# Four graph layers on one core: normalization moved to ScalarE, biases added within the gathering passes, and another order in the attention loop

## The chip, the cores and the metric

One NeuronCore of one Trainium2 chip. The time is that of one execution on the device, in microseconds (us). The kernel before took 5311.9 us, the median of three runs (5303.4 to 5312.3).

## The reference, cut to what matters

Four graph layers on 6,250 nodes with 128 features and 100,000 edges sorted by `dst`, each followed by a layer norm of x plus the layer's result:

```python
x = _layernorm(x + gat(x, ...))     # attention: softmax over the edges of each dst, weighted sum of h[src]
x = _layernorm(x + cfconv(x, ...))  # filters from edge_attr_128, messages, segment sum, two dense layers
x = _layernorm(x + gcn(x, ...))     # normalized sum of neighbours, + bias
x = _layernorm(x + gin(x, ...))     # (sum of neighbours + x) through two dense layers, + bias

def _layernorm(x, eps=1e-05):
    return (x - mean(x)) / sqrt(var(x) + eps)

# cfconv
f = ssp(edge @ We1 + be1) @ We2 + be2        # ssp(x) = softplus(x) - log 2
agg = segment_sum(xn[edge_index[1]] * f, edge_index[0])
return node + ssp(agg @ W2 + b2) @ W3 + b3   # so x + this = 2*node + ... + b3
```

## The kernel before, in words

Each engine has its own program (`vector`, `scalar`, `tensor`, `gpsimd`, `sync`), an in-order list of instructions; semaphores tie them together. The order of all work is written out by hand: a loop over ticks t, in which each engine works on several items, each with a lag behind t.

The nodes lie in 49 blocks of 128, the edges in 832 steps of up to 128 edges that share a block; four steps are a tick, so a pass over the edges has 208 ticks (`TICKS`). For the normalizing stages the blocks are grouped in 13 sets of four (`SETS`, `NS`; the last set has one block).

**Attention loop** (L802 to 815, L1155 to 1166, L1419 to 1428). GpSimd gathers rows of the table into a ring of 14 ticks (L1606 to 1612) and waits for `product_done` of 14 ticks earlier. VectorE has in each tick: `gat_top` (L663, the maximum of TensorE's masked bank), every fourth tick the chains `gat_max` (L673) and `gat_logit` (L715), `gat_sum` (L751, four dependent sums into `acc`), `gat_hot` (L742), `gat_turn` (L655), one or two steps of a background sort (`second_list`, L773), and last `f_plus_of` (L767), the sum that ends the softplus of the edge filters of the next layer. `weave` (L103) goes round these pieces, one step of each in a round, with a background step in the first and every third round. ScalarE has the background first, then `gat_dst`, `gat_weight`, `f_made_of`, `gat_weigh` and last `f_soft` (absolute value, exponential, logarithm). TensorE has the background first, then `gat_pair`, `gat_product`, `gat_mask`, `f_filter` and `f_hidden_of`. The filter chain is a ring over three engines: `f_hidden_of` (TensorE) waits for the last `f_plus_of`, `f_soft` for `f_hidden_of`, `f_plus_of` for `f_soft`.

At 14 places the background sort turns its keys over: TensorE transposes four 128x128 tiles into bank 3 (L1268), ScalarE copies them out (L1027), TensorE transposes four more after that copy, ScalarE copies again. On both engines that is one background step, so TensorE's second four stand at the head of its tick and wait for ScalarE's first copy. For the first 49 ticks ScalarE also counts in the background (L1015).

**Normalizing stages.** Per set, VectorE makes x plus the layer's result (`res`, a ring of four), its statistics (`stats_of`, L824) and later (lag 2) the normalization itself, `normed` (L832), one tensor_scalar per block; ScalarE makes 1/sqrt(var + eps) (`root`, L1168) as exponential of a logarithm. In stage 1 (L843) and stage 3 (L966) VectorE first adds the layer's bias row to x for the whole set (L850, L973). In stages 2 (L924) and 4 (L988) the result comes from two dense layers through TensorE and ScalarE (`turn`, `keep`, `times`, softplus or relu), and the bias of the second one is put into its bank by a matmul of a row of ones (L1444). In stage 1 TensorE then makes the table of the message stage from x, in stage 2 that of the third layer; stage 3's x goes to memory as the table of the fourth layer (L1794), and stage 4's is the output.

**The passes of layers 2 to 4** (`plain_layer`: L875, L1491, L1624). GpSimd gathers four times a tick, VectorE makes the hot blocks (L884), TensorE multiplies (L1498), VectorE adds the four products to the blocks' rows of `acc` (L872).

## Time and profile before

| | us |
|---|---|
| median of three runs | 5311.9 |
| the profiled execution | 5312.5 |
| its span, first to last instruction | 5310.7 |
| attention loop | 188 to 1391 |
| stage 1, normalization | 1391 to 1447 |
| message stage | 1447 to 1940 |
| pass of layer 2 | 1940 to 3003 |
| stage 2 | 3003 to 3072 |
| pass of layer 3 | 3072 to 4137 |
| stage 3 | 4137 to 4191 |
| pass of layer 4 | 4191 to 5257 |
| stage 4 | 5257 to 5311 |

Over the whole span TensorE's matmuls are busy 2721 us, VectorE 2760, ScalarE 1320, GpSimd 3525. These are averages over stages with different limits, so they name no limit of the whole. In rows of the trace, L12 is line 12 of the kernel, an arrow `<-` in brackets tells what ended the idle time before an instruction, PE is TensorE (PEld its weight loads), DVE VectorE, ACT ScalarE, POOL GpSimd. Instructions of a kind that follow each other closely stand in one row with their count (x4).

### The profile page before, as it was taken

How to read it: one execution, taken by the hardware profiler on the slowest of the kernel's cores; microseconds unless marked ns; L12 is line 12 of the kernel's file. 1: busy time of each engine (PE TensorE's matmuls, PEld its weight loads, DVE VectorE, ACT ScalarE, POOL GpSimd, SP SyncE). 2: the span in 40 equal slices, each digit the busy share in tenths (PEclk: the TensorE clock that was granted, in tenths of full speed). 3: DMA queues.
4: the chain of work that ended last, by engine and by line, in shares of the span. 5: the costliest groups of instructions: out<-in, count | busy, mean ns of one | idle time of the engine just before them, and what ended most of it. 6: DMA issues, size and time to landing. Idle time of an engine off the chain costs nothing. (4 is left out here: it accounts for less than half of the span.)

```text
span 5310.7 us, 54159 instructions
## 1 busy us (share of the span) xinstructions
PE 2721.2 (51%) x13301; PEld 2238.2 (42%) x13381; DVE 2760.1 (52%) x7383; ACT 1319.8 (25%) x3951; POOL 3524.7 (66%) x3833
## 2 busy tenths in 40 slices
PE   1477767777588864443333644434443244444445
PEld 1356555556466653333333433333333133333333
DVE  2699888888788863333333533333333533333334
ACT  4587666667366630000000200000000000000001
POOL 0677666767255557777777467777777377777773
PEclk8798898989677765555555655555555555555556
DMA  4666666667376742221111122212223222222224
GB/s 75 175 168 166 150 155 157 161 155 172 33 227 221 230 151 53 53 53 51 52 51 50 40 61 53 52 50 53 53 53 51 52 53 52 51 52 52 53 53 50
DMA packets 430927, 489.97 MB, mean 92 GB/s; under 512 B 86459, under 2 KB 333071, under 8 KB 430614
## 3 DMA queue, kind: packets, MB, share of 16 engines
q0 software_dynamic: 131904, 288.49, 23.2%
q1 hardware_dynamic: 295828, 197.27, 13.4%
q8 instruction: 116, 1.90, 0.2%
q10 hardware_dynamic: 2882, 0.70, 0.1%
q14 instruction: 197, 1.61, 0.1%
HBM read 359.63 MB, written 126.50 MB: 92 GB/s over the span
## 5 line engine op out<-in xcount | busy, mean ns | idle before, releaser
L1498 PE MATMUL bank<-arena 128*128 128x128 f32 x4992 | 1277.1, 438 | 1968.8 <-DVE arena L884 1690.8
L1572 POOL DMA_INDIRECT arena<-node_table,pick x1664 | 1593.0, 957 | 650.7 <-issue 507.2
L1498 PEld LDWEIGHTS bank<-arena 128*128 128x128 f32 x4992 | 1111.4, 328 | 2134.3 <-DVE arena L884 1863.8
L872 DVE TENSOR_TENSOR acc<-acc,bank 128x128 f32 x2496 | 719.1, 288 | 2101.7 <-PE bank L1498 1810.5
L1572 POOL DMA_INDIRECT arena<-gat_table,pick x832 | 856.3, 1029 | 348.2 <-issue 237.4
L1572 POOL DMA_INDIRECT arena<-message_table,pick x832 | 803.9, 966 | 255.8 <-issue 253.3
L1179 ACT COPY xt<-bank 128x512 f32<-128x512 f32 (+1 forms) x39 | 21.6, 554 | 2131.8 <-PE bank L1438 2131.7
L884 DVE TENSOR_TENSOR arena<-iota_free,local 128x512 f32<-128x512 f32 x624 | 428.0, 686 | 3.4 <-issue 2.4
L1487 PE MATMUL bank<-arena 128*128 x1664 | 338.4, 367 | 46.9 <-DVE arena L898 40.7
L1487 PEld LDWEIGHTS bank<-arena 128*128 128x128 f32 x1664 | 290.2, 263 | 114.2 <-issue 114.2
L763 DVE SCALAR_TENSOR_TENSOR acc<-acc,arena,bank 128x129 f32 x832 | 287.4, 345 | 66.0 <-DVE acc L763 34.1
L1171 ACT ACTIVATE rstd<-moments,eps_col 128x4 f32<-128x4 f32 (+1 forms) x52 | 15.5, 299 | 1158.3 <-DVE moments L829 1158.1
L1202 ACT ACTIVATE arena<-arena 128x128 bf16<-128x128 f32 x832 | 257.7, 310 | 153.6 <-DVE arena L906 133.8
L1391 PEld LDWEIGHTS bank<-arena 128*128 128x128 f32 x1664 | 260.3, 229 | 78.4 <-issue 70.1
L1391 PE MATMUL bank<-arena 128*128 128x129 f32 x1664 | 275.0, 318 | 7.5 <-ACT arena L1127 4.1
L1127 ACT ACTIVATE arena<-arena 128x128 f32<-128x128 f32 x832 | 265.4, 392 | 34.4 <-DVE arena L746 34.4
L1648 POOL DMA_DIRECT2D arena<-filter_table x208 | 112.5, 541 | 228.7 <-DVE arena L898 176.8
L1408 PE MATMUL bank<-xt,w_L_gnn_We 128*128 128x512 f32 x262 | 156.1, 680 | 189.5 <-DVE arena L769 188.7
L1400 PEld LDWEIGHTS bank<-w_L_gnn_We,arena 128*128 128x128 f32 x1568 | 219.3, 202 | 17.4 <-issue 7.0
L1400 PE MATMUL bank<-w_L_gnn_We,arena 128*128 128x128 f32 x1568 | 216.8, 283 | 11.6 <-ACT arena L1149 5.8
L898 DVE TENSOR_TENSOR arena<-bank,arena 128x512 f32<-128x512 f32 x208 | 143.8, 691 | 85.4 <-PE bank L1487 77.5
L769 DVE SCALAR_TENSOR_TENSOR arena<-bank,neg_L_gnn_be,arena 128x512 f32<-128x512 f32 x196 | 146.1, 746 | 79.5 <-ACT arena L1143 78.7
(219 smaller groups left out, 3373.2 us busy)
## 6 DMA issues: line engine op xcount, KB each, us to landing
message_table<-arena POOLq DMA_DIRECT2D x208, 256.0 KB, 3.3
filter_table<-arena SPq DMA_DIRECT2D x196, 256.0 KB
arena<-filter_table SPq DMA_DIRECT2D x624, 64.0 KB
xt<-edge_cols SPq DMA_DIRECT2D x131, 256.0 KB
arena<-local_rows SPq DMA_DIRECT2D x208, 128.0 KB
arena<-node_table,pick POOLq DMA_INDIRECT x1664
arena<-edge_cols SPq DMA_DIRECT2D x65, 256.0 KB
arena<-gat_table,pick POOLq DMA_INDIRECT x832
```

The costliest lines, as they stand in the source:

```text
L763: e.scalar_tensor_tensor(a, a, small["scale"][:, g % 2, q + s:q + s + 1], sum_place(t, s), ALU.mult, ALU.add).then_inc(summed, 1)
L769: e.scalar_tensor_tensor(magn[u % 2][:, :], bank[0][:, :], neg_col["L1_gnn_be1"][:, 0:1], magn[u % 2][:, :], ALU.max, ALU.add).then_inc(f_ ...
L872: e.tensor_tensor(a, a, bank[6 + t % 2][:, s * P:(s + 1) * P], ALU.add).then_inc(sums, 1)
L884: e.tensor_tensor(hot[n % 2][:, :, :], iota_free[:, :].unsqueeze(1).to_broadcast([P, GRP, P]), local[which][:, i:i + GRP].unsqueeze(2).to_ ...
L1127: ins = e.activation(hot[t % 3][:, s, :], hot[t % 3][:, s, :], ACT.Copy, scale=weight[:, s:s + 1])
L1202: e.activation(hot_copy[:, :], hot_n[n % HN][:, s * P:(s + 1) * P], ACT.Copy, accum_out=degree_part[:, i:i + 1]).then_inc(degree_added, 1)
L1391: ins = e.matmul(sum_place(t, s), hot[t % 3][:, s, :], gathered[:, slot(t, s), 0:D + 1], start=True, stop=True)
L1400: ins = e.matmul(bank[1][:, s * P:(s + 1) * P], magn[u % 2][:, s * P:(s + 1) * P], mats["L1_gnn_We2"][:, :], start=True, stop=True)
L1408: e.matmul(bank[0][:, :], mats["L1_gnn_We1"][:, :], edge_t[u % 3][:, :], start=True, stop=True).then_inc(f_hidden, 1)
L1487: ins = e.matmul(spread_bank(n)[:, s * P:(s + 1) * P], hot_n[n % HN][:, s * P:(s + 1) * P], xn[:, bass.ds(b, 1), :].rearrange("p o d -> p ...
L1498: ins = e.matmul(bank[6 + n % 2][:, s * P:(s + 1) * P], hot[n % 2][:, s, :], gathered[:, slot(n, s), 0:D], start=True, stop=True)
L1572: e.indirect_dma_start(out=dst, out_offset=None, in_=table, in_offset=bass.IndirectOffsetOnAxis(ap=index, axis=0)).then_inc(done, 16)
```

## The change

- `normed` moves from VectorE to ScalarE in all four stages: out of (res - mean) * rstd becomes Identity(res * rstd + shift), with shift = -mean * rstd made by VectorE for the whole set (`shift_of`, in the place where `normed` was, one 128x4 operation). The lags of what follows grow by one tick in stages 1 and 2.
- The bias rows of layers 2, 3 and 4 are added to x by VectorE within the pass before the stage that needs them (`add_row`, one operation per set, every eighth tick from tick 4). For layer 2 it is half of the row, since the stage takes x twice. The bias matmuls of stages 2 and 4 and the bias addition of stage 3 go. The first layer's bias addition (L850) stays.
- As x now changes within the last pass, VectorE waits for the writes of the fourth layer's table before it begins that pass.
- Attention loop: `f_plus_of` is a piece of `weave`, with one empty step first, so that it comes behind the second sum; ScalarE's tick begins with `f_soft` and `f_made_of`, and the background comes last. TensorE's tick is as before.

```diff
@@ vector, setup
-            e.tensor_tensor(out_row[:, :], bank[4][:, P:2 * P], rows["L1_gnn_b3"][:, :], ALU.add
-                            ).then_inc(fold_taken, 1)
+            q = own(e.tensor_tensor(out_row[:, :], bank[4][:, P:2 * P], rows["L1_gnn_b3"][:, :], ALU.add))
+            after(q)
+            e.tensor_scalar(half_row[:, :], out_row[:, :], 0.5, None, ALU.mult).then_inc(fold_taken, 1)
@@ vector, attention loop
             def f_plus_of(u):
+                yield
                 e.wait_ge(f_log, u + 1)
...
+                if 0 <= t - 3 < FTICKS:
+                    pieces.append(f_plus_of(t - 3))
                 weave(pieces, background, background_turns(t))
-                if 0 <= t - 3 < FTICKS:
-                    run(f_plus_of(t - 3))
@@ vector, normalizing stages
-            def normed(n, rs, x):
+            def shift_of(n, rs):
+                b0, b1 = span(n)
                 e.wait_ge(rs, n + 1)
-                for k, b in enumerate(SETS[n]):
-                    ins = e.tensor_scalar(x_sb[:, b, :], res[n % 4][:, k, :], moments[:, b, 0:1], rstd[:, b:b + 1],
-                                          ALU.subtract, ALU.mult)
-                ins.then_inc(x, 1)
+                e.scalar_tensor_tensor(shift[:, b0:b1], moments[:, b0:b1, 0], -1.0, rstd[:, b0:b1], ALU.mult, ALU.mult
+                                       ).then_inc(shifted, 1)
+
+            def add_row(n, row):
+                b0, b1 = span(n)
+                return own(e.tensor_tensor(x_sb[:, b0:b1, :], x_sb[:, b0:b1, :],
+                                           row[:, :].unsqueeze(1).to_broadcast([P, b1 - b0, D]), ALU.add))
...
-            def plain_layer(which, base):
+            def plain_layer(which, base, row):
                 for t in range(TICKS + 4):
+                    if t % 8 == 4 and t // 8 < NS:
+                        added = add_row(t // 8, row)
...
                 e.wait_ge(plain_summed, base + STEPS)
+                after(added)
...
@@ vector, stage 3 and the pass of layer 4
-                    q = own(e.tensor_tensor(xb[n % 2][:, 0:b1 - b0, :], x_sb[:, b0:b1, :],
-                                            rows["L2_gnn_b"][:, :].unsqueeze(1).to_broadcast([P, b1 - b0, D]),
-                                            ALU.add))
-                    after(q)
...
-                                                       xb[n % 2][:, k, :], ALU.mult, ALU.add))
+                                                       x_sb[:, b, :], ALU.mult, ALU.add))
...
-            plain_layer(0, 2 * STEPS)
+            e.wait_ge(table_out, 2 * 16 * NS)
+            plain_layer(0, 2 * STEPS, rows["L3_gnn_b2"])
@@ scalar, attention loop
             for t in range(TICKS + 13):
-                weave([], background, background_turns(t))
+                for lag, fn in ((3, f_soft), (5, f_made_of)):
+                    if 0 <= t - lag < FTICKS:
+                        fn(t - lag)
                 for lag, fn in ((4, gat_dst), (9, gat_weight)):
                     if (t - lag) % GT == 0 and 0 <= t - lag < TICKS:
                         fn((t - lag) // GT)
-                for lag, fn in ((5, f_made_of), (10, gat_weigh), (3, f_soft)):
-                    if 0 <= t - lag < (TICKS if fn is gat_weigh else FTICKS):
-                        fn(t - lag)
+                if 0 <= t - 10 < TICKS:
+                    gat_weigh(t - 10)
+                weave([], background, background_turns(t))
@@ scalar, normalizing stages
+            def normed(n, stage, x):
+                e.wait_ge(shifted, stage * NS + n + 1)
+                for k, b in enumerate(SETS[n]):
+                    ins = e.activation(x_sb[:, b, :], res[n % 4][:, k, :], ACT.Identity, scale=rstd[:, b:b + 1],
+                                       bias=shift[:, b:b + 1])
+                ins.then_inc(x, 1)
...
-            for t in range(NS + 8):
-                n = t - 7
+            for t in range(NS + 9):
+                n = t - 8
...
+                n = t - 3
+                if 0 <= n < NS:
+                    normed(n, 0, n1_x)
...
@@ tensor, times
-            def times(n, bk, buf, mat, done, bias_row=None):
-                cnt = len(SETS[n])
-                if bias_row is not None:
-                    e.matmul(bk[:, 0:cnt * P], ones[0:1, :], bias_row[0:1, :].unsqueeze(1).to_broadcast([1, cnt, D]),
-                             start=True, stop=False)
-                for k in range(cnt):
+            def times(n, bk, buf, mat, done):
+                for k in range(len(SETS[n])):
                     ins = e.matmul(bk[:, k * P:(k + 1) * P], buf[n % 2][:, k * P:(k + 1) * P], mat[:, :],
-                                   start=bias_row is None, stop=(bias_row is None or k == cnt - 1))
+                                   start=True, stop=True)
```

ScalarE's `normed` stands at lag 8 in stage 2, 3 in stage 3 and 8 in stage 4; the other shifted lags follow the diff's pattern.

## Rows read from the trace of the kernel before

**Rows 1.** Stages: length, busy us (count) of PE, PEld, DVE, ACT, POOL; clock, DMA share, GB/s

```profile
188.00:1391.00 1203.00, 855.44 (x5544) 697.62 (x5624) 1017.82 (x2713) 820.55 (x1942) 833.70 (x810) 0.89 0.66 155
1391.00:1447.00 56.00, 26.54 (x149) 22.21 (x149) 49.64 (x212) 18.71 (x52) 10.40 (x21) 0.70 0.10 27
3040.00:3050.00 10.00, 10.00 (x62) 7.09 (x61) 8.91 (x32) 6.66 (x16) 0.00 (x0) 1.00 0.17 52
4137.00:4191.00 54.00, 0.00 (x0) 0.00 (x0) 50.65 (x212) 12.91 (x39) 0.23 (x1) 0.50 0.20 60
5257.00:5311.00 54.00, 45.54 (x199) 26.41 (x199) 36.20 (x160) 21.34 (x52) 0.00 (x0) 0.88 0.20 60
```

**Rows 2.** Timeline in a pass: start, length, engine, line, operation [idle before <- its end]

```profile
2240.08 0.94 POOL L1572 DMA_INDIRECT arena<-message_table,pick  x1 [0.30 <-issue]
...
2244.92 0.29 DVE L872 TENSOR_TENSOR acc<-acc,bank 128x128 f32 x1 [2.80 <-PE bank L1498]
```

**Rows 3.** Timeline, an ordinary tick of the attention loop

```profile
603.23 1.06 PE L1391 MATMUL bank<-arena 128*128 128x129 f32 x8
...
605.99 0.35 DVE L763 SCALAR_TENSOR_TENSOR acc<-acc,arena,bank 128x129 f32 x1 [0.15 <-DVE acc L763]
...
606.26 0.74 DVE L769 SCALAR_TENSOR_TENSOR arena<-bank,neg_L_gnn_be,arena 128x512 f32<-128x512 f32 x1
...
606.92 0.68 DVE L666 TENSOR_REDUCE arena<-bank 128x4 f32<-128x512 f32 x1
```

**Rows 4.** Waits in the attention loop: waiting <- releaser: us in total, times, longest

```profile
DVE arena L769 <- ACT arena L1143: 78.7, 40, 5.7
```

**Rows 5.** Timeline, the first turn of the sort, and the last one's wait

```profile
540.73 0.58 ACT L1027 COPY arena<-bank 128x512 f32<-128x512 f32 x1 [5.90 <-PE bank L1268]
541.37 0.66 PE L1268 MATMUL bank<-ident,arena 128*128 128x128 f32 x4 [0.68 <-ACT arena L1027]
...
544.21 0.68 ACT L1139 ACTIVATE arena<-bank,c_L_gnn_be 128x512 f32<-128x512 f32 x1
...
546.24 0.75 DVE L769 SCALAR_TENSOR_TENSOR arena<-bank,neg_L_gnn_be,arena 128x512 f32<-128x512 f32 x1 [5.50 <-ACT arena L1143]
546.68 1.28 ACT L1127 ACTIVATE arena<-arena 128x128 f32<-128x128 f32 x4
...
547.14 1.63 PE L1408 MATMUL bank<-arena,w_L_gnn_We 128*128 128x512 f32 x2 [2.16 <-DVE arena L769]
...
548.56 1.93 PE L1391 MATMUL bank<-arena 128*128 128x129 f32 x8
...
1108.15 0.75 DVE L769 SCALAR_TENSOR_TENSOR arena<-bank,neg_L_gnn_be,arena 128x512 f32<-128x512 f32 x1 [5.67 <-ACT arena L1143]
```

**Rows 6.** Waits of GpSimd in the attention loop, and its last one, by timeline

```profile
POOL arena L1572 <- PE bank L1391: 97.4, 52, 5.7
...
1176.88 0.94 POOL L1572 DMA_INDIRECT arena<-gat_table,pick  x1 [4.43 <-PE bank L1391]
```

**Rows 7.** Timeline, VectorE's work for one set in stage 3

```profile
4152.52 0.69 DVE L973 TENSOR_TENSOR arena<-x_sb,r_L_gnn_b 128x512 f32<-128x512 f32 x1
4153.24 1.14 DVE L980 SCALAR_TENSOR_TENSOR arena<-acc,inv_sqrt_deg,arena 128x128 f32<-128x128 f32 x4
4154.41 0.87 DVE L826 BATCH_NORM_STATS2 stats<-arena 128x6 f32<-128x128 f32 x4
4155.32 0.38 DVE L829 BATCH_NORM_AGGREGATE moments<-stats 128x2 f32<-128x6 f32 x4
4155.62 1.08 DVE L835 TENSOR_SCALAR x_sb<-arena,moments,rstd 128x128 f32<-128x128 f32 x4
```

**Rows 8.** Groups by line, VectorE in the attention loop: count | busy us, mean ns | idle before

```profile
L684 DVE SCALAR_TENSOR_TENSOR arena<-arena 128x16 f32<-128x16 f32 x52 | 8.6, 165 | 0.0
```

**Rows 9.** Timeline, VectorE's first work of the message stage

```profile
1446.93 2.07 DVE L906 TENSOR_SCALAR arena<-bank,iota_part 128x512 f32<-128x512 f32 x3 [5.01 <-PE bank L1474]
```

**Rows 10.** Timeline, a bias matmul of stage 4

```profile
5283.42 1.12 PE L1444 MATMUL bank<-r_L_gnn_b,ones 1*128 1x512 f32 x2
```

More of the change, by code:

```diff
@@ L202, in build_program @@
         out_row = sb("out_row", [P, D])
+        half_row = sb("half_row", [P, D])
         gcn_w = sb("gcn_w", [P, D])
@@ L337, in build_program @@
                                      "x", "xturned", "xkept", "third", "rows"))
-        table_out = [sem(f"table{k}_out") for k in (1, 2)]
+        table_out, shifted = sem("table_out"), sem("shifted")
         plain_hot, plain_product, plain_summed = sem("plain_hot"), sem("plain_product"), sem("plain_summed")
@@ L920, in vector @@
             e.wait_ge(acc_zeroed, NS + 1)
-            plain_layer(1, 0)
-            for t in range(NS + 12):
-                n = t - 11
+            plain_layer(1, 0, half_row)
+            for t in range(NS + 13):
+                n = t - 12
                 if 0 <= n < NS:
@@ L961, in vector @@
             e.wait_ge(n2_rows, NS)
-            e.wait_ge(table_out[0], 16 * NS)
-            plain_layer(0, STEPS)
+            e.wait_ge(table_out, 16 * NS)
+            plain_layer(0, STEPS, rows["L2_gnn_b"])
             for t in range(NS + 3):
@@ L1210, in scalar @@
             e.wait_ge(plain_summed, STEPS)
-            for t in range(NS + 12):
-                n = t - 9
+            for t in range(NS + 13):
+                n = t - 10
                 if 0 <= n < NS:
                     keep(n, third_buf, bank[5], n2_xturned, n2_third, n2_xkept)
+                n = t - 8
+                if 0 <= n < NS:
+                    normed(n, 1, n2_x)
                 n = t - 6
@@ L1515, in tensor @@
             e.wait_ge(plain_summed, STEPS)
-            for t in range(NS + 12):
-                n = t - 10
+            for t in range(NS + 13):
+                n = t - 11
                 if 0 <= n < NS:
@@ L1531, in tensor @@
                         e.wait_ge(n2_res, n)
-                    times(n, bank[4], nplus, mats["L1_gnn_W3"], n2_second, out_row)
+                    times(n, bank[4], nplus, mats["L1_gnn_W3"], n2_second)
                 n = t - 2
@@ L1556, in tensor @@
                         e.wait_ge(n4_res, n)
-                    times(n, bank[4], nplus, mats["L3_gnn_W2"], n4_second, rows["L3_gnn_b2"])
+                    times(n, bank[4], nplus, mats["L3_gnn_W2"], n4_second)
                 n = t - 2
```

33 lines of the change are left out of this document (19 added, 14 removed).

## The prediction

> **What bounds the kernel now.** I read the stages first [rows 1], because the change touches five of them and each has a limit of its own. Three aggregation layers of some 1,065 us each are not in the table; what paces them is in [rows 2]: GpSimd issues one gather every 1.24 us (0.94 busy, 0.30 between), four to a tick, 4.99 us, and never rests, while VectorE sits idle 2.80 us of each tick. So 3,120 of the 5,311 us are paced by gathers that the change doesn't touch. What it can move is the first layer (the attention loop, 1,203 us, VectorE busy 1,018) and the four stages that normalize (56, about 69, 54 and 54 us).
>
> In the attention loop VectorE is the limit for most ticks. [Rows 3] show the end of an ordinary tick: a sum (L763) lasts 0.35 us and stands idle 0.15 before it, since it waits for the sum before, so the second, third and fourth follow every 0.50 us; then the softplus sum (L769) and at once the next tick's maximum (L666). L666 came 4.85 us earlier too, and the tick has no other hole than these two. The larger holes are VectorE's waits for ScalarE's logarithm, 78.7 us in 40 places [rows 4]. Some 56 of them lie at the 14 turns of the background sort, the first and the last in [rows 5] (5.50 and 5.67 us): ScalarE opens its turn with the sort's copy, which waits 5.90 us for TensorE's transposes, and only then comes to its softplus. The loop's end is set otherwise. GpSimd last waits for a freed ring slot at 1176.88 [rows 6]; from there to its last gather it runs flat out, and then the loop only drains. A gain of VectorE before 1177 shortens GpSimd's waits (97.4 us in all, so it passes on), one behind it is worth nothing.
>
> In the normalizing stages VectorE is the limit of the first and third ([rows 1]: 49.6 of 56 and 50.7 of 54 us busy), TensorE of the second (10.00 of 10.00 us) and nearly of the fourth (45.5 of 54).
>
> **The attention loop.** Three edits. *The softplus sum in mid-turn.* It is put between the second and the third sum. In ticks with neither the maximum chain nor the logit chain (two of four) it fills a hole: before, third and fourth sum start 0.50 apart, the softplus sum 0.27 behind, the next maximum 0.66 behind that; after, 0.27, 0.66, 0.50, 0.27 in place of 0.50, 0.50, 0.27, 0.66, which is 0.23 us less. In the other ticks small operations fill the hole already: nothing. Between the loop's fill and 1177 us there are about 83 such ticks, less 7 that hold a turn: 76 x 0.23 = 17.5, with the turns' own ticks 18 us. Its cover is that the logarithm is ready in mid-turn: from one softplus sum to the next the chain is 0.75 for the sum, 1.2 for TensorE's hidden product, 2.03 for the softplus (544.21 to 546.24, [rows 5]), 4.0 in all, under the 4.6 of a shortened tick. While ScalarE also counts (the first 49 ticks) its own work of some 5 us still fits the 5.5 us ticks. Where the cover is gone each 0.1 us of lateness costs 18 us.
>
> *ScalarE's order.* The softplus goes first, the background last; the waits in which ScalarE stood for VectorE's hot block don't set the pace.
>
> *The turns.* I replay one from [rows 5], from the end of a softplus sum, F. TensorE makes the hidden product (to F+1.2) and its first four transposes (to 1.8). ScalarE makes the softplus at once (to 3.2), so the 5.50 us wait is gone: VectorE comes to its sum at 3.2 anyway. But ScalarE then copies the filters and weighs (546.24 to 547.96, 1.72 us: to 4.95) before it copies the sort's first half (0.58: to 5.5). TensorE, which still opens its own turn with the transposes, stands until then; behind it in its queue are the second four, the product and the mask, 2.25 us at the full clock (each of these groups spans about what the 1.06 us row of [rows 3] does): mask at F+7.8. VectorE has ended its turn at F+4.9 and needs that mask for the next maximum: it waits 2.9 us, and 0.3 for the following softplus. That is what the cheaper turns wait now (five of the 14, 2.26 to 3.14 us). So the wait moves from the logarithm to the mask. TensorE is now idle for 3.7 us in it (0.68 before, row 541.37), and behind a hole of 2.2 us the trace has the product at half clock: 1.93 against 1.06 us. If that befalls the chain behind the copy, the mask comes at 9.9 and the wait is 5.0 plus 1.1: 2.9 us more per turn. Bounds: 0 and 2.9 a turn, 0 and 41 us for 14. I take 1.0, 14 us, since a stretch at the lower clock begins late and covers only a part of that chain, and some turns see none.
>
> The Trainium skill, page "TensorE: Matmul & The Clock Gate", section "HAM oscillation — how this bites in real kernels", says that a loop whose waits interrupt the matmuls long enough finds the array at half clock behind every such wait. By it all 14 turns would pay; the trace has both outcomes behind holes under 3 us.
>
> Sum of the loop: -18 + 14 = -4 us.
>
> **First normalizing stage.** VectorE loses four normalizations a set (from their row to the next set's first row, 1.00 us [rows 7], of which 1.08 is busy) and gets one 128x4 operation, 0.17 busy by its nearest row [rows 8], 0.20 with its gap. The set falls from 4.10 to 3.30 us. ScalarE gets four Identity activations of 128x128; the nearest row is the weighing, four in 1.28 us [rows 5], at most 1.6 if each takes its lone 0.39. It had 18.7/13 = 1.4 a set, so 2.9: VectorE stays the limit. 11 full sets save 8.8 us. Against that the drain: VectorE used to end with the last normalization, and 5.01 us later the message stage began [rows 9]; now ScalarE has three sets to normalize and a turn more to run before its last copies, which I put at 5.3 us (3 x 1.28, and what a turn's two copies take). Gain 3.5 us (bounds 0 and 8.8).
>
> **Second.** The bias matmul goes (1.12 us by its like in [rows 10]), VectorE 0.8; the half row is added to x before, in the idle 2.80 us of [rows 2]: 13 additions of 0.68, 9 us in 208 ticks, hidden, and GpSimd's 0.94 doesn't change beside VectorE's work now. But ScalarE, 6.66 of 10 us in a tick of 4.77, 3.2 a set, gets 1.28 and with its gaps is at 4.7, what TensorE had. Early sets a little faster, drain one turn longer: +1 (bounds -3 and +6).
>
> **Third.** VectorE also loses the bias addition (0.72): of 4.10 us are left 1.17 + 0.91 + 0.30 + 0.20 = 2.6. ScalarE: 12.9/13 + 1.28 = 2.3 a set, still under it. Twelve sets at 1.5 us, 17.5; ScalarE's drain behind the last set costs 2.7. Gain 15 us (bounds 8 and 18). The next layer's hot blocks now wait for the table's writes, as the gathers do already: nothing. The bias additions of the last two layers lie in the idle stretches of [rows 2], 13 in each.
>
> **Fourth.** TensorE loses 1.05 of 3.44 us (its bias row returns every 3.44), VectorE falls to 2.2, ScalarE rises from 21.3/13 = 1.6 to 3.0 or 3.1 and becomes the limit. Eleven sets at 0.35, the first set 1.0 sooner, and the last sets, which VectorE made at 3.05, at some 2.4: 6.5 us (bounds 2 and 9).
>
> Setup gets one dependent row operation, 0.3 us. Sum: -4 - 3.5 + 1 - 15 - 6.5 + 0.3 = -27.7. The profiled execution took 5312.5 us (span 5310.7 and 1.8 around it), 0.6 above the median of the runs: 5312.5 - 27.7 = 5285, and 5284 against the median; I give 5285.
>
> **Rivals.**
> *The clock holds* (or a lower one misses the chain): the turns cost nothing, 5285 - 14 = 5271; for it, some stalls before kept the full clock. 0.2.
> *The turns' wait simply goes*, as it would if nothing but the logarithm were late: another 56 us less, 5215. Against it: TensorE's transposes stand first in its queue and wait for the copy. 0.04.
> *Every turn pays the lower clock*: 5271 + 41 = 5312, no change. For it, the idle of 3.7 us is longer than any that a turn had on TensorE before. 0.15. (The page named above would have it so.)
> *Normalizing on ScalarE is dearer*, 1.6 a set and with waits between, and the bound of the third stage: 8 there, nothing in the first, +4 in the second: 5300. 0.1.
> *Slower*: the logarithm isn't ready when VectorE reaches the sum in mid-turn. The place is L769's new one; the price 0.1 us = 18 us over 182 ticks, on top of all turns at 41. It decides from 0.07 us a tick (13 us) on; at 0.2 us the time is 5312 + 36 = 5348. For it: TensorE must run product, mask and filter before the hidden product. Against it: 0.6 us of slack, and L666, which needs TensorE's mask in the same way, is seldom late before 1177. 0.09.
> *The forecast*: 0.42; by its own bounds 5272 to 5302.
>
> 0.2% of this kernel, 10.6 us, is about what a measurement can tell from no change. Below 5301: the forecast, the first two rivals, half of the dearer ScalarE: 0.42 + 0.24 + 0.05 = 0.71. Within: the other half and most of every turn paying, 0.19. Above 5323: the slower case and what is left of that one, 0.10. The range 5262 to 5318 leaves out the 5215, the slower case and the tails.
>
> **What would show it.** L769 no longer waits at the turns; L666 waits for L1370 there, 3 to 6 us, 14 times; if L666's wait is under 1 us there, the replay is wrong. Ordinary ticks of 4.62 instead of 4.85 us. Waits of L769 in ordinary ticks would mean the slower case. GpSimd's waits for freed slots should shrink by about what the loop gains. In the third stage the set takes 2.6 us and VectorE is busy nearly all of it; if it takes over 3, ScalarE is the limit. In the fourth 3.1 us with ScalarE busy. The three gathering layers keep 4.99 us a tick; if they don't, the additions weren't hidden.

## The result, and the profile after

| | before | after |
|---|---|---|
| median of the runs | 5308.2 us (4 runs) | 5252.7 us (4 runs) |
| the profiled execution | 5312.5 | 5251.8 |
| attention loop, first hot block to the division | 1202.6 | 1185.8 |
| stage 1 | 56.2 | 50.1 |
| message stage and pass of layer 2 | 1556.1 | 1539.3 |
| stage 2 | 68.9 | 69.6 |
| pass of layer 3 | 1064.9 | 1065.8 |
| stage 3 | 53.9 | 37.8 |
| pass of layer 4 | 1065.8 | 1066.8 |
| stage 4, last sum to ScalarE's last operation | 49.5 | 44.2 |

The ratio is 0.9898, interval 0.9881 to 0.9915: 55 us less by the medians, where I had forecast 28. The stages did what the sum said. The loop gained 16.8 us, not 4, and 17 us went in a stretch to which I gave nothing.

An ordinary tick of the loop after, by VectorE's timeline, with neither chain in it, answers to [rows 3] (columns as there):

```profile
404.65 0.35 DVE L765 SCALAR_TENSOR_TENSOR acc<-acc,arena,bank 128x129 f32 x1
404.91 0.75 DVE L772 SCALAR_TENSOR_TENSOR arena<-bank,neg_L_gnn_be,arena 128x512 f32<-128x512 f32 x1
405.57 0.34 DVE L765 SCALAR_TENSOR_TENSOR acc<-acc,arena,bank 128x129 f32 x1
406.06 0.35 DVE L765 SCALAR_TENSOR_TENSOR acc<-acc,arena,bank 128x129 f32 x1 [0.15 <-DVE acc L765]
406.33 0.69 DVE L668 TENSOR_REDUCE arena<-bank 128x4 f32<-128x512 f32 x1
```

The softplus sum (L772) stands behind the second sum, 0.26 us after its start, the third 0.66 behind it, then 0.49 and 0.27 to the maximum: the replay of the plain tick was right. From the maximum before (401.72) to this one it is 4.61 us.

A turn of the sort after, by the timeline of three engines, answers to [rows 5]:

```profile
622.79 0.60 PE L1295 MATMUL bank<-ident,arena 128*128 128x128 f32 x4
...
625.04 0.75 DVE L772 SCALAR_TENSOR_TENSOR arena<-bank,neg_L_gnn_be,arena 128x512 f32<-128x512 f32 x1 [0.73 <-ACT arena L1149]
625.38 1.28 ACT L1133 ACTIVATE arena<-arena 128x128 f32<-128x128 f32 x4
...
626.56 0.56 ACT L1033 COPY arena<-bank 128x512 f32<-128x512 f32 x1
...
627.17 1.11 PE L1295 MATMUL bank<-ident,arena 128*128 128x128 f32 x4 [3.78 <-ACT arena L1033]
...
628.08 1.93 PE L1418 MATMUL bank<-arena 128*128 128x129 f32 x8
...
630.32 0.38 PE L1397 MATMUL bank<-arena,far 128*128 128x512 bf16 x1
...
630.73 0.69 DVE L668 TENSOR_REDUCE arena<-bank 128x4 f32<-128x512 f32 x1 [2.92 <-PE bank L1397]
```

This is the wait that the prediction moved from the logarithm to the mask, with its 3.7 us of idle TensorE (3.78) and a product of 1.93 us behind it, for 1.06. The window of this product has a granted clock of 0.51, the lower of the two levels:

```profile
628.10:630.00 1.90, 1.90 (x11) 1.90 (x11) 0.00 (x0) 0.59 (x1) 0.00 (x0) 0.51 0.50 78
```

The waits of the loop say the same; they answer to [rows 4] and [rows 6]:

```profile
DVE arena L772 <- ACT arena L1149: 40.3, 39, 4.0
DVE arena L668 <- remote: 36.2, 11, 5.2
DVE arena L668 <- PE bank L1397: 33.2, 11, 4.6
POOL arena L1595 <- PE bank L1418: 62.7, 20, 12.9
```

A maximum released by "remote" or by L1397 is the same wait. It comes at all 14 turns, 50.8 us together, 3.6 each. GpSimd's waits for slots went from 97.4 to 62.7 us. That is 35 us, twice what the loop gained, since 9.8 us of it came back as time between gathers (waits <- issue, 231.0 before and 240.8 after) and 7.7 us as busy time of GpSimd (833.7 and 841.4).

In stage 3 a set takes 2.42 us on VectorE (two L985 rows apart), and the L838 row overlaps its neighbours but for 0.05 us. They answer to [rows 7]:

```profile
4104.93 1.13 DVE L985 SCALAR_TENSOR_TENSOR arena<-acc,inv_sqrt_deg,x_sb 128x128 f32<-128x128 f32 x4
4106.09 0.87 DVE L829 BATCH_NORM_STATS2 stats<-arena 128x6 f32<-128x128 f32 x4
4107.00 0.38 DVE L832 BATCH_NORM_AGGREGATE moments<-stats 128x2 f32<-128x6 f32 x4
4107.29 0.13 DVE L838 SCALAR_TENSOR_TENSOR shift<-moments,rstd 128x4 f32<-128x4 f32 x1
4107.34 1.13 DVE L985 SCALAR_TENSOR_TENSOR arena<-acc,inv_sqrt_deg,x_sb 128x128 f32<-128x128 f32 x4
```

ScalarE's timeline in the same stage: four normalizations in 1.63 us, and no idle time between the steps of a set, which takes 2.48 us. So the two engines share the bound.

```profile
4112.44 0.29 ACT L1179 ACTIVATE rstd<-moments,eps_col 128x4 f32<-128x4 f32 x1
4112.77 0.20 ACT L1181 ACTIVATE rstd<-rstd 128x4 f32<-128x4 f32 x1
4112.88 1.63 ACT L1186 ACTIVATE x_sb<-arena,shift,rstd 128x128 f32<-128x128 f32 x4
4114.42 0.60 ACT L1255 COPY acc<-x_sb 128x512 f32<-128x512 f32 x1
4114.93 0.29 ACT L1179 ACTIVATE rstd<-moments,eps_col 128x4 f32<-128x4 f32 x1
```

The windows of stages 1 and 4 after (columns as in [rows 1], to which they answer); in the fourth ScalarE is busy 38.1 of 44.2 us and TensorE 31.2:

```profile
1372.70:1422.80 50.10, 22.79 (x149) 19.16 (x149) 38.35 (x177) 37.37 (x101) 10.94 (x22) 0.80 0.12 33
5202.00:5246.20 44.20, 31.21 (x173) 22.33 (x173) 25.43 (x125) 38.09 (x101) 0.00 (x0) 0.89 0.22 66
```

### The profile page after: what moved, and what is told of

The parts are those of the page before. It is cut to its first block and busy times, and to the rows that moved or that the text cites. A ratio compares the mean times of both kernels' runs of the same rounds, so it can differ in the third digit from the quotient of the medians.

```text
span 5250.1 us, 54126 instructions
## 1 busy us (share of the span) xinstructions
PE 2666.8 (51%) x13249; PEld 2170.1 (41%) x13329; DVE 2713.8 (52%) x7266; ACT 1382.6 (26%) x4147; POOL 3523.0 (67%) x3833
## 5 line engine op out<-in xcount | busy, mean ns | idle before, releaser
L1521 PEld LDWEIGHTS bank<-arena 128*128 128x128 f32 x4992 | 1111.3, 328 | 2108.3 <-DVE arena L893 1795.0
L1595 POOL DMA_INDIRECT arena<-message_table,pick x832 | 792.5, 952 | 255.8 <-issue 253.2
L1510 PEld LDWEIGHTS bank<-arena 128*128 128x128 f32 x1664 | 281.4, 256 | 113.5 <-issue 113.5
L1427 PE MATMUL bank<-w_L_gnn_We,arena 128*128 128x128 f32 x1568 | 230.2, 292 | 184.3 <-ACT arena L1155 182.2
L1427 PEld LDWEIGHTS bank<-w_L_gnn_We,arena 128*128 128x128 f32 x1568 | 203.2, 200 | 233.4 <-issue 230.9
L1418 PEld LDWEIGHTS bank<-arena 128*128 128x128 f32 x1664 | 241.4, 214 | 78.1 <-issue 53.0
L1418 PE MATMUL bank<-arena 128*128 128x129 f32 x1664 | 256.0, 303 | 8.3 <-ACT arena L1133 3.7
L1145 ACT ACTIVATE arena<-bank,c_L_gnn_be 128x512 f32<-128x512 f32 x196 | 134.5, 686 | 302.8 <-PE bank L1435 302.7
L668 DVE TENSOR_REDUCE arena<-bank 128x4 f32<-128x512 f32 x208 | 142.4, 685 | 69.5 <-remote 36.2
```

The costliest lines, as they stand in the source:

```text
L668: e.tensor_reduce(small["top"][:, t // GT % 2, q:q + GRP], bank[2][:, :].rearrange("p (s n) -> p s n", s=GRP), AX.X, ALU.max).then_inc(max ...
L1418: ins = e.matmul(sum_place(t, s), hot[t % 3][:, s, :], gathered[:, slot(t, s), 0:D + 1], start=True, stop=True)
L1427: ins = e.matmul(bank[1][:, s * P:(s + 1) * P], magn[u % 2][:, s * P:(s + 1) * P], mats["L1_gnn_We2"][:, :], start=True, stop=True)
L1510: ins = e.matmul(spread_bank(n)[:, s * P:(s + 1) * P], hot_n[n % HN][:, s * P:(s + 1) * P], xn[:, bass.ds(b, 1), :].rearrange("p o d -> p ...
L1521: ins = e.matmul(bank[6 + n % 2][:, s * P:(s + 1) * P], hot[n % 2][:, s, :], gathered[:, slot(n, s), 0:D], start=True, stop=True)
L1595: e.indirect_dma_start(out=dst, out_offset=None, in_=table, in_offset=bass.IndirectOffsetOnAxis(ap=index, axis=0)).then_inc(done, 16)
```

## The experiments

To compare loops I cut them by the starts of the maxima: the first 12 ticks (fill), the next 37 (in which ScalarE still counts), the 70 ordinary ones of ticks 49 to 169, the 51 that lie within one tick before and two behind one of the 14 turns, and the end from tick 170 on. All in us; some 30 us of each loop lie outside the maxima.

| kernel | fill | next 37 | 70 ordinary | 51 at turns | end | loop |
|---|---|---|---|---|---|---|
| before | 57.4 | 204.4 | 395.0 | 325.5 | 190.7 | 1202.6 |
| after | 63.2 | 197.3 | 377.5 | 328.3 | 190.0 | 1185.8 |
| after, once more | 58.7 | 197.3 | 377.2 | 327.9 | 190.6 | 1181.3 |
| stages only | 58.0 | 205.1 | 396.9 | 325.2 | 192.0 | 1206.9 |
| sum in mid-turn only | 57.4 | 201.9 | 386.7 | 322.6 | 191.8 | 1190.0 |
| ScalarE's order only | 58.8 | 206.3 | 397.5 | 349.5 | 191.6 | 1233.3 |
| sum one step later | 59.0 | 197.5 | 375.2 | 331.3 | 190.4 | 1183.0 |
| turn kept busy | 60.6 | 197.3 | 377.0 | 303.4 | 189.5 | 1157.3 |
| sort's copies early | 61.2 | 197.2 | 377.3 | 299.6 | 189.2 | 1154.1 |
| copy of the filters first | 55.3 | 197.2 | 375.8 | 317.9 | 189.9 | 1165.7 |
| halves apart | 60.2 | 197.6 | 376.8 | 289.9 | 190.3 | 1144.4 |
| halves apart, sort's copies early | 61.8 | 197.4 | 381.7 | 269.9 | 201.8 | 1142.3 |
| halves apart, copy of the filters first | 54.4 | 197.4 | 379.3 | 276.3 | 202.4 | 1139.5 |
| halves apart, both copies early | 54.2 | 197.5 | 379.8 | 273.8 | 201.4 | 1136.4 |

### The change in parts, on a disturbed chip

Four kernels: before with both loop edits, with the sum in mid-turn alone (the diff's `f_plus_of` and `pieces.append` lines), with ScalarE's new order alone (the diff of ScalarE's loop), and after with both loop edits undone.

> The kernel before with only the two loop edits (softplus sum in mid-turn, softplus first on ScalarE). The two traces say that the loop's 16.8 us came about as follows: ordinary ticks of every kind 0.25 us shorter, 107 of them outside the turns' surroundings, and the turns and the loop's fill a few us dearer. If that is the work of these two edits, the loop here takes 1186 us and the kernel 17 us less than before; the four stages keep 56, 69, 54 and 50 us. My prediction's price list (76 ticks only, nothing in ticks with a maximum or logit chain) would give -4 us. On the 17 us that went between the message stage's start and the end of the second layer's pass: if they are an effect of the bias additions or of the stages, this kernel has 1556 us there as before; if that stretch varies from one execution to the next, it may show anything from 1539 to 1560.

> Only the softplus sum in mid-turn; ScalarE still opens its tick with the sort's background. If the ordinary ticks' gain comes from the sum's new place alone, they are 0.25 us shorter here too from tick 50 on. In the first 49 counting ticks and at the 14 turns ScalarE brings the logarithm as late as before, and VectorE now meets it two sums earlier: about 1 us more per turn, 14 us, and some 0.5 us in each counting tick. I expect the loop at 1180 to 1205, near 1195. If instead the order on ScalarE were what shortens the ordinary ticks, the ticks after 50 would keep 4.84 us and this loop would take over 1203.

> Only ScalarE's new order; the softplus sum stays at the end of VectorE's turn. If the wait at the turns only moves from the logarithm to the mask, as the prediction's replay has it, the maximum waits 2.5 to 5 us at each of the 14 turns, the softplus sum none, and the loop takes 1203 plus or minus 6 us; ordinary ticks keep 4.84 us. If the turns' wait were gained in full and the mask's wait came from the sum in mid-turn, the loop would take about 1150.

> The kernel after with both loop edits undone: only normalization on ScalarE and the biases in the passes. If the parts add up, stage 1 takes 50.0, stage 2 69.6, stage 3 37.8 and stage 4 44.2 us as after, the loop 1203 as before, and the kernel is 27 to 29 us faster than before, plus what the stretch of message stage and second pass does: 17 us more if the additions or the stages cause it, nothing on average if it varies by itself.

On this chip the kernel before took 5920.9 us. The four ratios to it were 1.0023 (1.0011 to 1.0035), 0.9979 (0.9968 to 0.9991), 1.0040 (1.0025 to 1.0055) and 0.9958 (0.9945 to 0.9970). The timeline of the first kernel in the pass of layer 2 shows why I put little on them: VectorE, GpSimd and TensorE stood still together.

```profile
2501.68 0.29 DVE L873 TENSOR_TENSOR acc<-acc,bank 128x128 f32 x1 [11.73 <-remote]
2501.79 0.94 POOL L1575 DMA_INDIRECT arena<-message_table,pick  x1 [4.75 <-remote]
...
2503.94 4.19 PE L1501 MATMUL bank<-arena 128*128 128x128 f32 x16 [11.86 <-DVE arena L885]
```

What causes these stops is not shown. Undisturbed plain ticks were 4.60 us with the sum in mid-turn and 4.84 or 4.85 without, whatever ScalarE's order; only with the sum in mid-turn and ScalarE's old order every second one took 5.28, which the next section takes up. The turns could not be read.

### The same parts on an undisturbed chip

> The kernel before with only the softplus sum in mid-turn, once more, on a chip without the common stops, where the turns can be read. In the disturbed execution the undisturbed ticks already measured 4.60, 5.52 and 5.96 us in place of 4.84, 5.88 and 6.12. So: ordinary ticks of all three kinds 0.25 us shorter on average after tick 50 (70 of them outside the turns: 395 to 377.5 us); in the 37 counting ticks as in the kernel before, within 3 us, if the logarithm is late there behind ScalarE's count; at the 14 turns the old wait for the logarithm, now in mid-turn, about 1 us dearer each than the 325 us of their 51 ticks before. Loop 1190 to 1205. If ScalarE's order were needed for the gain, the counting ticks would be longer than before by 0.3 us or more each.

> The kernel before with only ScalarE's new order, once more. Ordinary ticks 4.84 us as before. At the turns the maximum waits for the mask, 2.5 to 5 us, instead of the logarithm; the 51 ticks around the turns keep their 325 us within 10. In the first 12 ticks, in which the filters' ring of engines sets the pace, the filter product now waits for ScalarE's copy of the last filters, which comes behind the softplus instead of before it: 4.7 to 5.0 us a tick in place of 4.1 to 4.6, about 5 us in all. Loop 1203 to 1215. If the fill's 5.8 us came from the sum in mid-turn instead, nothing is seen there.

> The kernel after with the loop as before, once more. Stages 50.0, 69.6, 37.8 and 44.2 us as after; loop 1203 within 3 us; the kernel 27 to 29 us faster than before apart from what the three gathering passes do by themselves (the second pass's gathers took 1056 us in one kernel and 1045 in the other; if that is chance, this one may have either).

Measured: 0.9972 (0.9957 to 0.9987), 1.0046 (1.0029 to 1.0063) and 0.9948 (0.9928 to 0.9968), loops of 1190.0, 1233.3 and 1206.9 us. The stages alone gave 50.0, 69.6, 37.7 and 44.9 us: they are independent of the loop. They are worth 26 us here and 27 in the kernel after, where my sum had 24 for them (3.5 - 1 + 15 + 6.5).

The loop's two edits are not. The sum in mid-turn alone gains 12.6 us. Its turns wait 59.5 us for the logarithm (56 before), so the 1 us more per turn that I expected was not there. In ordinary ticks it is held up at 30 places by some 0.58 us, because ScalarE first waits for VectorE's hot block:

```profile
DVE arena L770 <- ACT arena L1144: 81.2, 49, 5.7
ACT arena L1116 <- DVE arena L739: 78.0, 37, 4.8
```

That is what ScalarE's order does. I had written that those waits "don't set the pace"; with the sum at the end of the turn they didn't, in mid-turn they do, and the order gives 9 us in the 70 ordinary ticks and 5 in the 37 before them.

ScalarE's order alone loses 30.7 us, 24 of them at the turns; I had expected none there, and 12 at most in all. A turn with the sum still at the end:

```profile
636.66 0.75 DVE L769 SCALAR_TENSOR_TENSOR arena<-bank,neg_L_gnn_be,arena 128x512 f32<-128x512 f32 x1 [0.34 <-ACT arena L1143]
...
643.46 0.79 PE L1270 MATMUL bank<-ident,arena 128*128 128x128 f32 x4 [3.78 <-ACT arena L1027]
...
644.04 1.93 PE L1393 MATMUL bank<-arena 128*128 128x129 f32 x8
...
647.28 0.69 DVE L666 TENSOR_REDUCE arena<-bank 128x4 f32<-128x512 f32 x1 [4.76 <-PE bank L1372]
```

The softplus sum (L769) from which the replay of the prediction counts ends at 637.4, and the maximum that waits for the mask starts at 647.3, 9.9 us behind it; with the lower clock paid the replay had the mask at 9.9. The 14 maxima wait 67.9 us, 4.8 each, against 3.6 in the kernel after.

### The place of the sum

After, with a second empty step in `f_plus_of`, so that the sum comes behind the third sum of the tick:

```diff
             def f_plus_of(u):
                 yield
+                yield
                 e.wait_ge(f_log, u + 1)
```

> The kernel after with the softplus sum between the third and the fourth sum instead of the second and the third. If the gain of the ordinary ticks is the hole that the sum fills, the plain ticks stay at 4.60 us here. The filters' ring then has 0.5 us less between a softplus sum and the next maximum, and the mask at the turns comes that much later for VectorE: some 0.5 us more at each of the 14 turns, 7 us. In mid-turn the logarithm is waited for 0.5 us less at some 16 places of ordinary ticks, 5 us back. Loop 1181 to 1192. Rival: it is the earlier hidden product that shortens the ticks; then plain ticks grow to 4.7 us or more and the loop takes over 1195.

0.9923 (0.9900 to 0.9946), loop 1183.0. Ordinary ticks gain as much as with the sum one step earlier (375.2 and 377.5 us for 70), so the gain is the hole and not an earlier ring. The maxima at the 14 turns wait 60.4 us, 4.3 each. So the further back the sum stands in VectorE's turn, the longer the wait for the mask: 3.6, 4.3 and, at the end, 4.8 us.

### The lower clock at the turns

After, with the first four transposes of each turn of the background sort made seven times, to the same places:

```diff
-                            for q in range(4 * h, 4 * h + 4):
+                            for q in (*range(4 * h, 4 * h + 4),) * (7 if i == 1 and not h else 1):
                                 ins = e.transpose(
```

> The kernel after, in which TensorE makes the first four transposes of each of the 14 turns seven times over (the same tiles to the same places), 24 transposes more, some 2.6 us of work in the 3.8 us in which it waits for ScalarE's copy. If the lower clock behind that wait is what each turn pays, the product behind it takes 1.06 instead of 1.93 us, the mask comes 1.5 to 2 us earlier, the maximum waits 1.6 to 2.2 us on average instead of 3.6, and the loop is 18 to 28 us shorter than the 1181 to 1186 of the kernel after, with more work in it. If the clock isn't what counts (or doesn't hold through the 1.2 us that are left idle), the loop stays within 4 us, or gets 5 us longer where the copy comes later.

0.9865 (0.9843 to 0.9888), loop 1157.3: with 24 transposes more per turn the 51 ticks at the turns take 303.4 us in place of 328. Its timeline at a turn:

```profile
602.86 3.22 PE L1295 MATMUL bank<-ident,arena 128*128 128x128 f32 x28
...
607.35 0.66 PE L1295 MATMUL bank<-ident,arena 128*128 128x128 f32 x4 [1.27 <-ACT arena L1033]
607.84 1.06 PE L1418 MATMUL bank<-arena 128*128 128x129 f32 x8
...
609.87 0.68 DVE L668 TENSOR_REDUCE arena<-bank 128x4 f32<-128x512 f32 x1
```

Its product has a granted clock of 1.00, the upper level:

```profile
607.80:608.90 1.10, 1.10 (x12) 1.10 (x11) 0.24 (x1) 0.59 (x1) 0.80 (x2) 1.00 0.61 88
```

Behind 1.27 us of idle time and four transposes the product takes 1.06 us; behind 3.78 us and the same transposes it took 1.93. Here all 14 products behind a copy take 1.06 or 1.14 us. In the kernel after ten take 1.93 us or more, three 1.34 to 1.56, and one, behind 3.89 us of idle time, 1.19. The maxima of that stretch wait 32.1 us at 12 places, in place of 50.8 at 14. So the lower clock costs the kernel after some 25 us at its 14 turns, 1.8 each on average. By the rule of the Trainium skill that the prediction cites (page "TensorE: Matmul & The Clock Gate", section "HAM oscillation — how this bites in real kernels") every turn pays. The trace agrees in the main: of the 14 turns of the kernel after ten pay in full, three in part and one hardly, and with ScalarE's order alone all 14 pay (1.93 us or more).

### Other orders at the turns

*Sort's copies early*: the first of these edits. *Copy of the filters first*: the second. *Halves apart*: TensorE's background step ends behind the first four transposes, and the second four come between the mask and the filter product, the third.

```diff
@@ scalar: sort's copies early
                 for lag, fn in ((3, f_soft), (5, f_made_of)):
                     if 0 <= t - lag < FTICKS:
                         fn(t - lag)
+                weave([], background, background_turns(t))
...
                     gat_weigh(t - 10)
-                weave([], background, background_turns(t))
@@ scalar: copy of the filters first
-                for lag, fn in ((3, f_soft), (5, f_made_of)):
+                for lag, fn in ((5, f_made_of), (3, f_soft)):
@@ tensor: halves apart
                             if h:
+                                split.append(1)
+                                yield
                                 e.wait_ge(sort_kept[i], n)
...
                 for lag, fn in ((11, gat_product), (2, gat_mask), (4, f_filter), (2, f_hidden_of)):
+                    if fn is f_filter and split:
+                        split.clear()
+                        next(background[1], None)
```

> The kernel after with ScalarE's background directly behind the filters' copy instead of at the end of its tick: the sort's copies at a turn come before the weighing, some 1.3 to 1.7 us sooner. My theory: VectorE's maximum at a turn waits (3.6 us on average over 14) for TensorE's mask, which waits for the copy; so each turn gets up to 1.5 us shorter, 14 turns about 15 to 20 us less than the kernel after, 5235. Rival: the wait is set by the chain softplus sum, hidden product, logarithm, or by the weighing that now comes later and that TensorE's product needs: then nothing is gained, or the 49 counting ticks lose some 0.3 us each: 5253 to 5265.

> The kernel after with ScalarE's copy of the filters before the softplus again, as it stood in the kernel before (the background stays last). If that copy behind the softplus is what makes the fill's ticks 5 us long instead of 4.1 to 4.6, the first 12 ticks fall from 63.2 to about 57 us, and TensorE's 182 us of waits for that copy shrink to a fraction, so that mask and hidden product come earlier. Loop 5 to 10 us shorter than 1186. Rival: the fill is slow because VectorE stands for the logarithm before it has made the hot block of the next mask; then nothing changes there, and the softplus may come up to 0.57 us later at every tick, of which 12 or more us would show.

> The kernel after with TensorE's second four transposes of a turn put between its mask and its filter product, so that product and mask no longer stand behind ScalarE's copy. My theory: the maximum's 3.6 us wait at 11 or so of the 14 turns (those that fall in ticks with one background step) goes; the filter and hidden products come up to 1.5 us later, of which the softplus sum then waits about 1. Net 2 to 3 us per turn, 25 to 40 us less than after: 5213 to 5228. Rival: the logarithm comes so much later that VectorE waits in mid-turn for what it no longer waits at the mask: no change from 5253.

> Both of the above. With the copy made when the second transposes come to it, the filter product isn't held up: my theory gives another 0.5 to 1 us per turn beyond the kernel with the halves apart alone, 5205 to 5220. Rival: ScalarE now stands at its second copy for TensorE's second transposes, which come behind product and mask, before it weighs; the next product and GpSimd's freed slots come later and it is no better than the halves apart alone, or worse.

> The kernel after with TensorE's second transposes put behind its mask (the halves apart, loop 1144 us) and ScalarE's copy of the filters before the softplus (alone a loop of 1166 us). If the two act on different waits, the loop takes 1130 to 1140 us and the kernel 5205 to 5225; GpSimd issues its gathers back to back in 832 x 1.33 = 1107 us or so and then sets the limit, so I do not expect less.

> The same with the sort's copies also early on ScalarE, before the weighing. The kernel with halves apart and early copies had a loop of 1142 us, in which TensorE's mask already waited 44 us for gathered rows, so GpSimd is near to being the limit there. I expect 1125 to 1140 us of loop, and no clear difference from the kernel without the early copies.

| kernel | median us | ratio to before |
|---|---|---|
| sort's copies early | 5237.0 | 0.9878 (0.9857 to 0.9899) |
| copy of the filters first | 5242.6 | 0.9889 (0.9865 to 0.9913) |
| halves apart | 5226.7 | 0.9858 (0.9837 to 0.9878) |
| halves apart, sort's copies early | 5227.3 | 0.9855 (0.9833 to 0.9878) |
| halves apart, copy of the filters first | 5202.5 | 0.9820 (0.9796 to 0.9844) |
| halves apart, both copies early | 5204.1 | 0.9839 (0.9807 to 0.9870) |

Both ways to bring the mask sooner shorten the turns alone, by 28 us (copies ahead of the weighing) and 38 us (halves apart). The first gained more than the 15 to 20 us that I expected. TensorE then stands idle 2.62 us at most of its turns instead of 3.78, and 5 of the 14 products behind a copy take 1.06 us; that is part of the rest, how much of it is not shown. With the copy of the filters first the loop is 16 to 20 us shorter, not the 5 to 10 that I expected: the fill is 55.3 us as its theory had it, but 10 us came from the turns, which I had not seen: the filter product waits for that copy behind the softplus at nearly every tick (waits in the loop of the kernel after):

```profile
PE bank L1427 <- ACT arena L1155: 182.2, 170, 7.6
```

Of the halves apart with the sort's copies early I had expected 5205 to 5220 us; it takes no less than the halves apart alone (5227.3 and 5226.7). The turns' ticks fall by another 20 us, to 269.9, but where the turns are fixed so far the end grows from 190 to some 202 us and the mask begins to wait for gathered rows. These are two waits of the halves apart with the sort's copies early, from 250 to 1170 us; the new one is the second:

```profile
POOL arena L1607 <- issue: 206.5, 677, 0.3
PE bank L1399 <- DMA arena<-gat_table,pick: 44.0, 35, 2.7
```

GpSimd then issues almost without a stop (in this window it waits 0.6 us for slots, 48.9 in the kernel after), and the bound passes to its gathers. The halves apart with the copy of the filters first has the lowest ratio, 0.982, where the kernel after has 0.990 and 0.994; from the one with both copies early it is not told apart (5202.5 and 5204.1 us, and the intervals overlap).

### The kernel after once more, and the gathering passes

> The kernel after, unchanged, beside the other three. The four kernels run before this ran on a chip on which all engines stand still together again and again for 3 to 20 us (before takes 5921 us there), so their ratios tell little. If this execution is free of that, before is near 5308 and this one near 5253 us, its loop 1186 us. The stretch from the message stage's start to the end of the second pass, 1556 us before and 1539 after: if it varies by itself, it is not 1539 within 2 us again; the gathers of the second pass, 1044.7 us from first to last, would lie anywhere between 1038 and 1056.

0.9940 (0.9921 to 0.9960), against 0.9898: by the medians 40 us less than before, not 55 (by the ratios 32 and 54), and the two intervals don't overlap. The profiles show the reason. Over the 14 undisturbed executions the message stage and the three passes together took between 3661.7 us (halves apart, both copies early) and 3697.5 us (halves apart alone), though those two have the same code there; the second pass alone took 1044 to 1062. The kernel before's profile has 3686.8, after's 3671.9, after once more 3680.5, ScalarE's order alone 3679.0, the stages alone 3666.4. Two windows of the kernel before, both within its second pass, show what varies:

```profile
2200.00:2400.00 200.00, 81.88 (x320) 71.27 (x320) 69.93 (x199) 0.00 (x0) 151.24 (x161) 0.50 0.20 53
2400.00:2600.00 200.00, 77.93 (x305) 67.88 (x306) 68.18 (x194) 0.00 (x0) 153.07 (x155) 0.50 0.20 51
```

For stretches of some 20 to 165 us a gather takes 1.33 us instead of 1.25, since about each fourth lasts 1.1 to 1.4 us instead of 0.94. From the first gather of the second pass to its last it is 1056.2 us before and 1044.7 after; 832 at 1.248 us are 1038.6, so at 0.08 us each some 220 gathers were slow before and 76 after, at other places. What brings them is open; that they are not the change's is shown by the kernels above, which have them with and without the bias additions.

## Why the prediction was wrong

The sum said 27.7 us. The measured parts, apart from the passes, are: loop -16.8 and -21.3 in two executions, stage 1 -6.2, stage 2 +0.7, stage 3 -16.2, stage 4 -5.3, setup -1.2 (it lies between 186.9 and 190.6 us in all 14 executions, so this is chance): 45 to 50 us. Two comparisons gave 55 and 40, around that, since the passes move by more than 10 us by themselves. I treated one profiled execution of the passes as if they were fixed. In the first comparison they were 15 us shorter in the profile after than in the one before, and both misses were needed to leave the range: without these 15 us the profiled execution is at 5267, inside 5262 to 5318, and the second comparison (5267.8) is inside too.

**The failed step** is the loop's term for VectorE's ticks, -18 us, which measured some -34. One part of it gave nothing without a reason: "In the other ticks small operations fill the hole already: nothing." They don't. A tick with the maximum chain, before (timeline of VectorE):

```profile
399.88 0.34 DVE L763 SCALAR_TENSOR_TENSOR acc<-acc,arena,bank 128x129 f32 x1
...
400.37 0.35 DVE L763 SCALAR_TENSOR_TENSOR acc<-acc,arena,bank 128x129 f32 x1
...
400.87 0.35 DVE L763 SCALAR_TENSOR_TENSOR acc<-acc,arena,bank 128x129 f32 x1
...
401.97 0.74 DVE L769 SCALAR_TENSOR_TENSOR arena<-bank,neg_L_gnn_be,arena 128x512 f32<-128x512 f32 x1
402.63 0.68 DVE L666 TENSOR_REDUCE arena<-bank 128x4 f32<-128x512 f32 x1
```

and the same tick after:

```profile
399.12 0.34 DVE L765 SCALAR_TENSOR_TENSOR acc<-acc,arena,bank 128x129 f32 x1
399.38 0.75 DVE L772 SCALAR_TENSOR_TENSOR arena<-bank,neg_L_gnn_be,arena 128x512 f32<-128x512 f32 x1
...
400.13 0.35 DVE L765 SCALAR_TENSOR_TENSOR acc<-acc,arena,bank 128x129 f32 x1
...
400.62 0.35 DVE L765 SCALAR_TENSOR_TENSOR acc<-acc,arena,bank 128x129 f32 x1
...
401.72 0.68 DVE L668 TENSOR_REDUCE arena<-bank 128x4 f32<-128x512 f32 x1
```

From the second sum to the next maximum it is 2.75 us before and 2.60 after: the small operations left part of the hole, and 0.15 us go. Over the 70 ordinary ticks those with a chain gained 0.12 and 0.13 us on average; those without gained 0.28 and 0.47, the latter behind the maximum chain. I had nothing and 0.23. So 107 ordinary ticks gained 24.6 us (17.5 + 7.1): 19.8 in the 54 without a chain, for which 0.23 each is 12.4, and 4.7 in the 53 with one. The larger miss is thus the size of the 0.23, which was 0.37. Of the 0.47 us behind the maximum chain 0.07 lie ahead of the second sum, where the hot block took 0.71 us before and 0.68 after and `gat_turn` 0.39 and 0.35; and in two of these 17 ticks the sum before waited for the logarithm, 0.35 and 1.07 us. By the same 0.25 us each the 37 ordinary ticks among the turns' 51 gained 9, an estimate: 34 us in all, where my term was 18.

**The turns** were priced at +14. The 51 ticks grew by 2.6 us on average of both executions; with the 9 us that the ordinary ones among them gained by the estimate, the 14 turns cost 12. The term is right by luck, since two errors cancel: I replayed with the softplus sum in its old place, at the end of VectorE's turn (its new place gives back 1.2 us of the mask's wait, 4.8 to 3.6), and I let the lower clock count for 1.0 us a turn, a third of the 2.9 that I had worked out for it, while the kernel kept busy shows 1.8. What was to be seen was there: L668 waits at all 14 turns, at 10 of them 3.1 to 5.2 us, at two 2.8 and 2.9, and at two 1.0 and 1.3.

**The fill** cost 1 to 6 us and had no term; the two executions of one kernel differ by 4.5 us there, and the copy behind the softplus accounts for 3 to 8.

**The stages** came out by their terms. *First*: 6.2 where 3.5 was said; the set fell to 3.14 us, not 3.30, because the shift costs 0.05 us beside its neighbours and not 0.20, and the drain cost 4.4 (11 x 0.96 - 6.2), not 5.3. *Second*: +0.7, said +1. *Third*: 16.2, said 15. *Fourth*: 5.3, said 6.5, ScalarE's set 3.02. ScalarE's four normalizations take 1.63 to 1.66 us, a little over the upper bound that I had named (1.6), and not the 1.28 of the weighing. The forecast held in stage 3 only because 2.48 us on ScalarE is still near VectorE's 2.42. **The bias additions** were hidden, as said: gathers stay at 1.25 us.

**The rivals.** None of them gave the time. The slower case's place, L772 in ordinary ticks, waits in the fill (12 times, 16 us; L769 before 8 times, 10 us) and behind tick 170, where GpSimd sets the end; between them, away from the turns, once for 0.1 us. Around the turns it waits 10.5 us in 16 places, where L769 waited 56. "The clock holds" is refuted by the 1.93 us products and the kept-busy turn. "Every turn pays the lower clock" was right in its condition at 13 of the 14 turns, but its price of 41 us was 25. "Normalizing on ScalarE is dearer" had the 1.6 us a set right and the bound of the third stage in part, but that stage gained 16 us, not 8.

## What to carry to other kernels

Where one engine's in-order list sets the pace, moving an independent operation between two dependent ones pays in every tick, also where smaller operations already stand between them: measure the distance between the fixed points before and after it, not the marked idle time. When a wait is moved to another engine, replay it from the place where its start now stands, and let TensorE pay the lower clock behind idle stretches of the length that the trace shows it paid; then look whether its own order lets it do the awaited work first. Before a profile of a gathering pass is used as a constant, compare several executions: here 36 us in 3680 came and went.

## What the runs showed of the hardware

- 24 repeated transposes in each of 14 waits of TensorE, most of them of 3.8 us, made the loop of the kernel after 24 to 29 us shorter: the 128x129 products behind these waits ran at the upper level of the clock (granted 1.00 instead of 0.51, 1.06 instead of 1.93 us at the turn shown). The length of the idle time alone does not tell the clock: behind 3.78 us a product took 1.93 us, behind 3.89 another took 1.19.
- The gathers (indirect DMA issued by GpSimd) have stretches of some 20 to 165 us with 1.33 us each instead of 1.25.
- One chip showed common stops over the whole kernel: behind the setup 84 to 86 per execution of 2.5 to 10 us in which none of four engines worked, some 335 us, and longer ones of single engines (VectorE up to 20 us). Before takes 5921 us there, 11% more than the 5295 to 5308 in the median of the other batches.
- An Identity activation of 128x128 with a column for scale and one for bias took 0.41 us in a run of four (1.63), a weighing with a column for scale alone 0.32 (1.28).
